# Attention on one Trainium2 core: the projections of a batch moved nearer to its scores, and the small steps around them reordered

## The reference

```python
x = x + tanh(g_xattn[0]) * xattn(layernorm(x), ctx, Wq, Wk, Wv)
x = x + tanh(g_ffn[0]) * ffn(layernorm(x), ...)

def xattn(x, context, Wq, Wk, Wv):
    q = x @ Wq.T;  k_raw = context @ Wk.T;  v_raw = context @ Wv.T
    kv = concat([k_raw, v_raw], -1).reshape(b, m, 32, 16, 2)
    q, k = rmsnorm(q), rmsnorm(kv[..., 0]);  v = kv[..., 1]
    return softmax(q @ k.T * 16 ** -0.5) @ v

def ffn(h, ...):
    # one of 8 experts a row (top 1 of x @ router_w.T), gated by a sigmoid,
    # w_gate_up[e] (512 x 2048), silu(g) * u, w_down[e] (1024 x 512),
    # plus one shared expert of the same shapes for all rows
```

## Time and profile before

| | before |
|---|---|
| median of 3 runs | 1104.04 us (1103.55 to 1106.19) |
| the profiled execution, its time | 1103.48 us |
| its span | 1101.4 us |
| mean granted clock of TensorE | 0.977 |
| TensorE busy | 1047.0 us (95%) |
| VectorE busy | 603.8 us (55%) |
| ScalarE busy | 568.7 us (52%) |
| GpSimd busy | 169.3 us (15%) |

### The profile page before, as it was taken

How to read it: one execution, slowest core, us unless ns; L and a number is a source line. 1 busy time by engine, 2 the same in 40 slices (tenths; PEclk the granted TensorE clock), 3 DMA queues, 4 the chain that set the end, 5 groups by cost and what they waited for, 6 DMA issues and landing times. The chain is left out here.

```text
span 1101.4 us, 26510 instructions
## 1 busy us (share of the span) xinstructions
PE 1047.0 (95%) x11645; PEld 852.4 (77%) x11645; DVE 603.8 (55%) x1187; ACT 568.7 (52%) x862; POOL 169.3 (15%) x170
## 2 busy tenths in 40 slices
PE   4889999999999999999669999999999999999997
PEld 3667777777777777776458788888888999999996
DVE  4774455644446554553447644434447666666663
ACT  4356766766676676667543221212125555555552
POOL 0000111101111111111322220000011212333111
PEclk9999999999999999999669999999999999999999
DMA  7400000000000000000113120101038777787762
GB/s 231 104 8 29 30 29 29 30 20 11 29 30 29 29 29 29 2 2 2 43 32 126 50 69 20 39 20 36 15 119 247 233 219 232 231 233 221 214 206 77
DMA packets 62170, 93.14 MB, mean 85 GB/s; under 512 B 5378, under 2 KB 43266, under 8 KB 62048
## 3 DMA queue, kind: packets, MB, share of 16 engines
q1 hardware_dynamic: 53544, 74.90, 22.4%
q0 software_dynamic: 5664, 13.18, 3.9%
q10 hardware_dynamic: 2840, 3.29, 1.0%
HBM read 82.24 MB, written 10.29 MB: 84 GB/s over the span
## 5 line engine op out<-in xcount | busy, mean ns | idle before, releaser
L371 PE MATMUL bank<-arena_f32r 128*128 128x512 f32 (+2 forms) x1344 | 367.5, 411 | 16.7 <-DVE arena_f32r L692 16.6
L371 PEld LDWEIGHTS bank<-arena_f32r 128*128 128x128 f32 (+2 forms) x1344 | 228.4, 182 | 76.0 <-DVE arena_f32r L692 11.4
L584 ACT ACTIVATE probs<-score_banks 128x1600 f32<-128x1600 f32 x96 | 144.7, 1507 | 81.6 <-PE score_banks L407 81.6
L1141 ACT ACTIVATE hT_hi<-arena_f 128x224 fp32r<-128x224 f32 (+1 forms) x96 | 42.2, 440 | 165.7 <-DVE arena_f L1148 165.7
L736 POOL TENSOR_TENSOR k_pack<-normed,k_pack 128x512 f16<-128x512 f32 (+1 forms) x45 | 52.5, 1166 | 417.2 <-ACT k_pack L566 417.2
L706 DVE TENSOR_REDUCE sumsq<-arena_f 128x32 f32<-128x512 f32 (+1 forms) x64 | 43.8, 684 | 132.7 <-ACT arena_f L536 132.7
L422 PE MATMUL bank<-probs,values 128*17 128x100 f32 (+1 forms) x3072 | 89.2, 259 | 10.8 <-ACT probs L584 10.8
L422 PEld LDWEIGHTS bank<-probs,values 128*17 128x17 f32 (+1 forms) x3072 | 65.7, 100 | 43.3 <-issue 30.6
L1123 PE MATMUL bank<-arena_f32r 128*128 128x224 f32 (+1 forms) x672 | 93.6, 298 | 0.8 <-DVE heads_out L751 0.8
L1123 PEld LDWEIGHTS bank<-arena_f32r 128*128 128x128 f32 x672 | 91.1, 193 | 2.4 <-DVE heads_out L751 1.2
L1148 DVE TENSOR_TENSOR arena_f<-bank,arena_f 128x224 f32<-128x224 f32 (+1 forms) x96 | 43.1, 449 | 76.1 <-PE bank L1123 76.1
(11 more groups left out here) (176 smaller groups left out, 1819.3 us busy)
## 6 DMA issues: line engine op xcount, KB each, us to landing
arena_f<-L_ffn_w_gate_up SPq DMA_DIRECT2D x32, 512.0 KB, 4.6
w_raw<-L_ffn_w_gate_up SPq DMA_DIRECT2D x32, 512.0 KB, 4.2
arena_f<-ctx SPq DMA_DIRECT2D x15, 722.0 KB, 4.2
w_raw<-L_ffn_w_down SPq DMA_DIRECT2D x16, 512.0 KB, 4.5
arena_f<-L_ffn_w_down SPq DMA_DIRECT2D x16, 512.0 KB, 3.9
x_all<-x SPq DMA_DIRECT2D x4, 800.0 KB
gated_rows<-arena_f POOLq DMA_DIRECT2D x16, 200.0 KB, 3.6
x_rows<-x_all ACTq DMA_DIRECT2D x4, 800.0 KB
```

Source lines behind the costliest of these rows:

```text
L371: product = PE.matmul(bank[0:rows, :], k.srcT[t % 2][a][:, j, 0:rows], weight, start=(m == 0), stop=(m == 11))
L584: A.activation(k.probs[n % 2][:], k.score_banks[:, :, 0:GH * k.N].rearrange("p j (r n) -> p j r n", r=GH), ACT.Exp, scale=float(HD) ** -0. ...
L1141: A.activation(k.hT[it % 2][0][:, j, 0:width], k.hidden[j][:, 0:width], ACT.Copy).then_inc(r.h_high, 1)
```

## The change

It does these things:

- A batch's projections begin at slot 24 * (b - 2) + 15 (`prep_start`) in place of 24 * (b - 2). Two places replace the one of before: j counts from the start of a batch's projections (up to 40 slots), i from the start of its scores (also up to 40). The slots begin at -41.
- Queries are the fifth product of the seven; the last two are values and keys of the third context tile. The tiles therefore have a new order, 0, 1, 3, 2 (`PLACE`, `TILE`).
- The inverse roots are computed in three groups: context tiles 0 and 1 together, queries, tile 2, at j = 16, 19 and 27, each in the same 11 instructions on 64, 32 and 32 columns.
- The eight turning events of bank 0 stand three slots apart: in slots (modulo 24) 0 x source, 3 pack of tile 2, 6 and 9 the output halves of the batch before, 12 and 15 packs of tiles 0 and 1, 18 and 21 the query halves. The outputs of a batch are so turned 6 and 9 slots after its last row has begun; those of the last batch at 14 and 27.
- Weighted values stand one slot later (`PV_SLOT` = 3), so behind the next unit's scores. Scores need four of the five turned packs, all five only for tile 2.
- The low part of the packs is POOL's for the first batch too.
- x is loaded and normalised in five parts, of batches 0, 1 to 3, 4 to 7, 8 to 11 and 12 to 15; x of batch 0 is the first transfer of SP. The layer norm of the first part is worked off at once; the others stand at slots -14, 4, 28 and 52. The chunks of x1 stand at 96 * (c + 1) + 12 (the last at + 6).
- The routing of the first chunk begins at slot 361 in place of 355.

```diff
-SRC_SLOTS = (-3, 0, 9, 17)
-WEIGHT_SLOTS = (-55, -48, -47, -47, -40, -39)
-RMS_SLOT = 25
-PACK_SLOTS = (6, 8, 11, 14)
-PACK_T_SLOTS = ((9,), (11,), (15,), (19, 21))
-PV_SLOT = 2
-OUT_SLOTS = (13, 25)
-X1_SLOT = 8
+LEAD = 15
+PLACE = (0, 1, 3, 2)
+TILE = (0, 1, 3, 2)
+VALUE_AT = (0, 2, 5)
+HEADS_AT = (1, 3, 6, 4)
+PROJECTION_TILE = (0, 0, 1, 1, 3, 2, 2)
+SRC_SLOTS = (-3, 0, 9, 13)
+WEIGHT_SLOTS = (-7, 0, 1, 1, 12, 13)
+RMS_SLOTS = (16, 19, 27)
+RMS_TILES = (slice(0, 2), slice(3, 4), slice(2, 3))
+RMS_OF = (0, 0, 2, 1)
+PACK_SLOTS = (18, 20, 31, 22)
+PACK_T_SLOTS = ((21,), (24,), (36,), (27, 30))
+PACK_T_AT = (0, 1, 4, 2)
+PV_SLOT = 3
+X_PARTS = ((0, 1), (1, 4), (4, 8), (8, 12), (12, 16))
+X_SLOTS = (None, -14, 4, 28, 52)
+ROUTE_SLOT = 361
...
-def windows(k, s):
-    return [(it, s - 24 * it) for it in (s // 24 - 1, s // 24, s // 24 + 1) if -2 <= it < k.B]
+def preparing(k, s):
+    return [(b, s - prep_start(b)) for b in range(k.B) if -4 <= s - prep_start(b) < 40]
+
+def prep_start(b):
+    return 24 * (b - 2) + LEAD
+
+def out_slots(k, b):
+    return (30, 33) if b + 1 < k.B else (14, 27)
+
+def scoring(k, s):
+    return [(b, s - 24 * b) for b in range(k.B) if 0 <= s - 24 * b < 40]
...
 def taken_slot(i):
-    return max(projection_end(i) + 1, PACK_SLOTS[0] + 1) if i == 1 else projection_end(i) + 1
+    return projection_end(i) + 1
...
 def pe_attention(k):
...
+        for b, j in preparing(k, s):
+            if j == SRC_SLOTS[2]:
+                pe_turn_source(k, PE, w, b)
+            for n in range(84):
+                if n * 24 // 84 == j:
+                    pe_project(k, PE, w, b, n)
+            for t in range(4):
+                for half in range(len(PACK_T_SLOTS[t])):
+                    if j == PACK_T_SLOTS[t][half]:
+                        pe_turn_pack(k, PE, w, b, t, half)
+        for b, i in scoring(k, s):
+            for z in range(2):
+                if i == out_slots(k, b)[z]:
+                    pe_turn_outputs(k, PE, w, b, z)
+            for u in range(6):
+                if i == 4 * u + PV_SLOT:
+                    pe_weighted_values(k, PE, w, b, u // 3, u % 3)
...
 def pe_scores(k, PE, w, s):
-    w.wait_ge(k.kt_copied, 5 * b + 5)
+    w.wait_ge(k.kt_copied, 5 * b + (5 if t == k.NMT - 1 else 4))
...
 def dve_attention(k):
...
+        for c in range(len(X_PARTS)):
+            if c:
+                dve_layer_norm(k, V, w, 0, c, s - X_SLOTS[c])
+            elif s == k.first_slot:
+                for step in range(CT + 2):
+                    dve_layer_norm(k, V, w, 0, 0, step)
+        for b, j in preparing(k, s):
+            for p in range(4):
+                if j == SRC_SLOTS[p] + 2:
+                    dve_source_low(k, V, w, b, TILE[p])
+            if j == SRC_SLOTS[2] - 2:
+                dve_normalise_x(k, V, w, b)
+            for n in range(7):
+                if j == taken_slot(n) + 1 and n not in VALUE_AT:
+                    dve_sum_squares(k, V, w, b, PROJECTION_TILE[n])
+            for g in range(3):
+                if j == RMS_SLOTS[g]:
+                    dve_rms(k, V, w, b, g)
+            for t in range(4):
+                if j == PACK_SLOTS[t]:
+                    dve_scale(k, V, w, b, t)
+        for b, i in scoring(k, s):
+            for z in range(2):
+                dve_finish(k, V, w, b, z, i - out_slots(k, b)[z] - 1)
...
-def dve_rms(k, V, w, b):
-    s = k.sumsq[b % 2][:]
-    before = RMS_EVENTS * b
-    w.wait_ge(k.summed, 4 * b + 4)
+def dve_rms(k, V, w, b, g):
+    tiles = RMS_TILES[g]
+    s, root, tmp = (t[:, tiles, :] for t in (k.sumsq[b % 2], k.rms[b % 2], k.rms_tmp))
+    before = RMS_EVENTS * (3 * b + g)
+    w.wait_ge(k.summed, 4 * b + 2 + g)
     V.tensor_scalar(s, s, 1.0 / HD, RMS_EPS, MULT, ADD).then_inc(k.rms_v, 1)
-    w.wait_ge(k.scaled, 4 * (b - 2) + 4)
+    w.wait_ge(k.scaled, 4 * (b - 2) + 2 + g)
     for step in range(RSQRT_STEPS):
         w.wait_ge(k.rms_v, before + step + 1)
-        rsqrt_step(V, k.rms[b % 2][:], k.rms_tmp[:], s, step).then_inc(k.rms_v, 1)
+        rsqrt_step(V, root, tmp, s, step).then_inc(k.rms_v, 1)
...
 def sp_attention(k):
     SP, w = k.SP, Waits(k.SP)
+    sp_load_x(k, SP, 0)
     sp_load_weights(k, SP, w, 0, 0)
...
     sp_load_context(k, SP, w, 0, slice(1, None))
-    sp_load_x(k, SP, 0)
     for half in range(2):
         sp_load_weights(k, SP, w, 2, half)
-    for b in range(1, k.B):
+    sp_load_context(k, SP, w, 1)
+    for c in range(1, len(X_PARTS)):
+        sp_load_x(k, SP, c)
+    for b in range(2, k.B):
         sp_load_context(k, SP, w, b)
```

More of the change, by code:

```diff
@@ L30 @@
 RSQRT_STEPS = 10
-LN_EVENTS = 2 * 4 + 1 + RSQRT_STEPS
 RMS_EVENTS = 1 + RSQRT_STEPS
@@ L201, in lay_out_semaphores @@
 def lay_out_semaphores(k, sem):
-    k.x_in = [sem(f"x_in{i}") for i in range(4)]
+    k.x_in = [sem(f"x_in{i}") for i in range(len(X_PARTS))]
     k.ctx_in = [sem(f"ctx_in{i}") for i in ("_even", "_odd", "_rest")]
@@ L279, in turn_order @@
     for s in range(k.first_slot, k.last_slot):
[L280 to L284, removed]
+        for b, j in preparing(k, s):
+            order += [("src", b)] if j == SRC_SLOTS[2] else []
+            order += [("pack", b, t, half) for t in range(4) for half in range(len(PACK_T_SLOTS[t]))
+                      if j == PACK_T_SLOTS[t][half]]
+        for b, i in scoring(k, s):
+            order += [("out", b, z) for z in range(2) if i == out_slots(k, b)[z]]
     return order, {name: n for n, name in enumerate(order)}
@@ L305, in pe_attention @@
             pe_scores(k, PE, w, s + 1)
[L306 to L325, removed]
+        for b, j in preparing(k, s):
[15 more added lines that the diff above has]
+                    pe_weighted_values(k, PE, w, b, u // 3, u % 3)
+        if s == ROUTE_SLOT - 1:
             pe_turn_router(k, PE, w)
-        if 355 <= s < 355 + ROUTE_STEPS:
-            pe_route(k, PE, w, 0, s - 355)
+        if 0 <= s - ROUTE_SLOT < ROUTE_STEPS:
+            pe_route(k, PE, w, 0, s - ROUTE_SLOT)
     return w
@@ L477, in act_attention @@
-        if s == 354:
+        for b, j in preparing(k, s):
+            for p in range(4):
+                if j == SRC_SLOTS[p] + 1:
+                    act_source_high(k, A, w, b, TILE[p])
+            for n in range(7):
+                if j == taken_slot(n):
+                    if n in VALUE_AT:
+                        act_copy_values(k, A, w, b, PROJECTION_TILE[n])
+                    else:
+                        act_take_heads(k, A, w, b, PROJECTION_TILE[n])
+            for t in range(4):
+                if j == PACK_SLOTS[t] + 1:
+                    act_pack_high(k, A, w, b, t)
+                for half in range(len(PACK_T_SLOTS[t])):
+                    if j == PACK_T_SLOTS[t][half] + 1:
+                        act_copy_pack(k, A, w, b, t, half)
@@ L483, in act_attention @@
+        if 0 <= s - ROUTE_SLOT - ROUTE_STEPS < 2:
+            act_part_high(k, k.first, A, w, s - ROUTE_SLOT - ROUTE_STEPS)
     return w
@@ L661, in dve_weight_low, with ln_part, ln_done, dve_layer_norm @@
     V.tensor_tensor(low, src, high.bitcast(F32), SUB).then_inc(k.w_low, 1)
[L664 to L668 removed]
+def ln_part(x1, c):
+    return (CT * c, CT * c + CT) if x1 else X_PARTS[c]
+def ln_done(x1, c):
+    done = 0
+    for at in [(0, i) for i in range(len(X_PARTS))] + [(1, i) for i in range(4)]:
+        first, end = ln_part(*at)
+        done += 2 * (end - first) + 1 + RSQRT_STEPS
+        if at == (x1, c):
+            return done
+def dve_layer_norm(k, V, w, x1, c, step):
+    first, end = ln_part(x1, c)
+    before = ln_done(x1, c) - 1 - RSQRT_STEPS
+    if 0 <= step < end - first:
         if x1:
[L670 removed]
+            w.wait_ge(k.x1_made, 2 * end)
         else:
             w.wait_ge(k.x_in[c], 16)
[L673 to L674 removed]
+        V.bn_stats(k.ln_raw[:, first + step, :], k.x_all[:, first + step, :]).then_inc(k.ln_v, 1)
+    part = slice(first, end)
     if step == CT:
[L676 to L677 removed]
+        w.wait_ge(k.ln_v, before - (end - first))
+        for b in range(first, end):
             V.bn_aggr(k.ln_mv[:, b, :], k.ln_raw[:, b, :]).then_inc(k.ln_v, 1)
[L679 removed]
+        w.wait_ge(k.ln_v, before)
         V.tensor_scalar(k.ln_var[:, part], k.ln_mv[:, part, 1], LN_EPS, None, ADD).then_inc(k.ln_v, 1)
[L681 to L682 removed]
     if step == CT + 1:
[L684 to L685 removed]
+        for i in range(RSQRT_STEPS):
+            w.wait_ge(k.ln_v, before + 1 + i)
             rsqrt_step(V, k.ln_rstd[:, part], k.ln_tmp[:, part], k.ln_var[:, part], i).then_inc(k.ln_v, 1)
@@ L690, in dve_source_low @@
     src, high, low = source_views(k, b, t)
-    w.wait_ge(k.src_high, 4 * b + t + 1)
+    w.wait_ge(k.src_high, 4 * b + PLACE[t] + 1)
     V.tensor_tensor(low, src, high.bitcast(F32), SUB).then_inc(k.src_low, 1)
 def dve_normalise_x(k, V, w, b):
-    w.wait_ge(k.ln_v, LN_EVENTS * (b // CT + 1))
+    w.wait_ge(k.ln_v, ln_done(0, [c for c, (first, end) in enumerate(X_PARTS) if first <= b < end][0]))
     w.wait_ge(k.src_turned, b)
```

201 lines of the change are left out of this document (71 added, 130 removed).

## The result

The changed kernel takes 1121.36 us (median of 4 runs, 1119.9 to 1124.58), the kernel before 1105.12 in the same series (1103.55 to 1106.65). The ratio is 1.0151 with a 95% interval of 1.0121 to 1.0181: 16 us slower. Forecast were 1108.5 in a range of 1078 to 1118, so the side was right and the size was not: the time lies 3.4 us above the range. The profiled execution took 1122.42 us with a span of 1120.5.

What follows compares the result with a forecast made beforehand. PE was taken as full in the middle, idle at both ends. 46 + 469.0 + 18.2 + 9.6 + 3.5 + 1.2 + 34 = 581.5 against 577.03 at the shared stage, 4.5 later, gave 1108.5 us; range 1078 to 1118.

Steps and rivals of the forecast that it cites:

- the moved weighted values: Full middle on PE: operand changes from the new place cost 0, bounds -0.1 and +0.2 us a unit over 88 units.
- the rival: Middle: the clock falls in many batches or operand changes cost 0.1 us a unit, 7 to 10 us more; chance 0.12.
- The queue on DVE: Middle: DVE's work ahead of reading the second output half makes PE wait 1.3 us a batch, 18.2 over 14 batches.
- the straight line: DVE root steps, interpolated between 4 and 128 columns: 0.25 us on 64 columns, 0.22 on 32.
- the held step: Second root group on DVE: POOL's low-part pack of tile 0 holds one root step, 1.0 us more.
- half: Middle: POOL held in place of DVE, or queue 0.8 shorter; 0.5 us a batch, 1095 to 1098 us; chance 0.2.
- the queue fits: Middle: DVE's queue ends before 10.4 us, so turning tile 0 waits for nothing; 1084 us; chance 0.28.
- Layer norms and the clock: First batches: three x layer norm parts in DVE's queue cost 9.6 us, one fall of PE's clock 3.5.
- The chunks of x1: Slots 12 to 17: 0.7 us ahead of the scale of queries for three batches, taken as 1.2 us.
- The start: Up to the first scores: they come at 46 us in place of 63.9, with about 5 us of waiting.
- The tail: Slot 351 to the shared stage: 8 units left, 34 us, bounds 30 and 42.
- weighted values beside the exponential: Tail: weighted values no longer between the exponential and the next scores, 6.5 us less over 8 units.

Runs made afterwards that it cites:

- e8: Changed kernel with four steps in place of ten in each group of norm roots (roots less exact): 1086.83 us, ratio 0.9843.
- e11: Changed kernel with four root steps in place of ten, weighted values issued right behind their slot's scores, ahead of its projections: 1072.58 us.
- e9: Changed kernel with PV_SLOT back at 2, x layer norms at slots 17, 41 and 65, and four root steps in place of ten: 1073.91 us.
- e5: Changed kernel with PV_SLOT back at 2 and the last x layer norms at slots 17, 41 and 65: 1095.55 us.
- e3: Changed kernel with the root group of queries at j = 21 in place of 19: 1121.3 us.
- e6: Changed kernel with PV_SLOT 2, x layer norms at 17, 41 and 65, and the root group of queries at 21: 1100.87 us.
- e7: Changed kernel with VectorE's scoring steps, the readers of the turned output, ahead of the preparing steps of the same slot: 1121.19 us.
- e4: Changed kernel with the last three x layer norm parts at slots 17, 41 and 65 in place of 4, 28 and 52: 1113.07 us.
- e1: Changed kernel with weighted values back in slot 4u + 2, directly ahead of the next unit's scores: 1108.11 us.
- e2: Kernel before with only the weighted values moved to slot 4u + 3, behind the next unit's scores: 1116.93 us.
- e10: Kernel before with four steps in place of ten for its norm roots, as a control: 1097.45 us.
- e12: Changed kernel with PV_SLOT 2, x layer norms at 17, 41 and 65, and seven root steps in place of ten: 1084.06 us.

## Why the prediction was right or wrong

**The step that failed: the moved weighted values, taken as 0.** The prediction bounded it at -0.1 and +0.2 us a unit and took 0 "because the wait for the exponential moves with it". In the full middle there was no such wait to move. Measured are 1.14 to 1.16 us a period, 0.19 a unit (e8 against e11 and e9), at the upper bound: 88 units, 16.9 us. The sentence ahead of it had the reason why no value between the bounds was supported: no row showed weighted values followed by a projection. With the upper end the forecast would have been 1126; the bound was kept out of the range by giving operand changes a share of a chance of 0.12 and sizing them at 0.1 in the rival.

**The queue on DVE: right.** 1.3 us a batch were forecast. Taking the queue's load away won 1.07 (e8 against after) and 1.22 (e9 against e5). The root steps cost 0.25 and 0.22 as on the straight line, the held step 0.9 in place of 1.0. Seen as a wait of PE it is only 0.74 a period, because PE itself came later to it. That POOL's pack would hold DVE and not the reverse held in these rows, and "half" and "the queue fits" fell with it. The text summed the whole queue but put the wait at its one reader, the second output half; e3, e6 and e7 show that another order earns nothing, since the next thing in line is as late.

**Layer norms and the clock: right in kind.** 9.6 + 3.5 = 13.1 forecast; e4 took 11.6 us out of the three periods. The clock fell with a wait of 3.4 us as forecast (0.89 from 96 to 128 us), and once more with one of 3.3 (0.95 from 128 to 160), where the forecast had one fall. The chunks of x1 cost 0.87 in three periods, 2.6 us in place of 1.2.

**The start: right.** 46 forecast, 45.61 measured, with 4.2 us of waits for POOL's pack where 5 were taken.

**The tail: 34 forecast, 39.1 measured.** Its step of 8 x 0.81 = 6.5 us, weighted values beside the exponential, cannot be found in the runs. With the weighted values away from the scores the tail is shorter in three pairs, by 1.7 (e1, 40.8 against 39.1), 2.4 (e9, 38.2 against e8, 35.8) and 1.4 (before, 41.4, against e2, 40.0), but longer by 4.7 in the fourth (e5, 36.1, against e4, 40.8). e5 and e6 lie 6.0 apart with one group of roots moved, most of it with the clock. So the tail scatters by as much as the effect, and how the 5.1 us divide stays open. The window of the tail after has PE busy for 28.99 of 40 us at a clock of 0.73:

```profile
554.00:594.00 40.00, 28.99 (x646) 22.74 (x645) 20.87 (x66) 22.51 (x29) 13.70 (x25) 0.73 0.17 51
```

Its largest waits are 2.3 us for a copied output and 1.8 for a copied pack, both of ACT. What each of its waits and the clock cost was not tried.

**The sum.** Against the forecast of the shared stage at 581.5 it came at 593.38, 11.9 later: -0.4 at the start, +7.2 from the first scores to unit 88 (508.7 in place of 469.0 + 18.2 + 9.6 + 3.5 + 1.2 = 501.5), +5.1 in the tail. The middle's +7.2 hides larger parts: +16.9 for the cut projections; -4.4 for what is left of the period (33.9 less 1.15 and 1.07 is 31.68, 0.30 below the 31.98 that the forecast used, 14.7 times); -2.5 for the queue (1.07 taken 14.7 times is 15.7, not 18.2); -2.8 because the first period is that much shorter than a steady one (31.08 against 33.9 in e4); -1.5 for the layer norms of x and +1.4 for those of x1. They give 7.1. Behind the seam come 2.7 us for which the forecast had nothing. (The forecast's own arithmetic is a little loose in two rivals: 581.5 - 18.2 - 3.5 - 2 is 557.8, which gives 1085 and not 1084, and "half" gives 1094 to 1097; neither moves the range.)

**Its own tests.** The successor of L387 waited for that of L751 12 times by 500 us, most by 0.74 and not 1.2; the period was 33.9, not 33.3; batches came longer by 3 to 5 us. The forecast of 33.3 missed by just the operand changes, less what the new order wins.

## What to carry to other kernels

Where TensorE is full, an issue order that puts another kind of matmul between two small ones cost 0.19 us in every unit here though no view showed a wait: compare the spacing of starts, or the period, not the busy share. When a wait names the last reader of a buffer on a full queue, first shorten the queue or move work out of that stretch; a new order gives the wait another name. And where a term has no row, and the bounds times their count decide the sign, the range has to hold the worse bound together with the other costs, not in place of them.

## What the hardware showed that was not expected

Matmuls with nothing changed but their neighbours took longer: 14 projections took 3.53 us in two pieces around the weighted values and 3.34 in one piece, PE being busy at full clock in both. With the earlier trace rows alone that cannot be seen.

The same wait brought the clock down in some executions and not in others. From the shared stage's start to the end of the span before took 524.4 us and after 527.1, with the same work. 1.3 of the 2.7 are in its first 24 matmuls. The rest is in a second fall, 60 to 80 us into the stage, before and after:

```profile
637.03:657.03 20.00, 18.25 (x104) 16.50 (x104) 11.28 (x33) 3.54 (x6) 6.45 (x8) 1.00 0.30 94
653.38:673.38 20.00, 18.26 (x96) 16.30 (x95) 11.34 (x33) 3.98 (x7) 6.46 (x8) 0.91 0.23 69
```

In both PE waits 1.7 us there for VectorE; behind that wait the clock fell only in the changed kernel. The fourteen profiles divide by this fall: without it (before, e3, e8, e10, e11, e12) the stage took 524.3 to 524.4 us, with it 525.9 to 527.9. It isn't the entry alone: e2 had its first 24 matmuls in 4.64 us, the shortest, had the fall and took 525.9. What decides whether the clock falls, no run shows.

A small step on VectorE (0.19 us) with two operands in SBUF, beginning 0.12 us behind a pack of POOL, was held until that pack's end (1.09 us), once in each batch. The Trainium skill says in SBUF — State Buffer, section "Who interferes with whom", that the order of issue decides who blocks; POOL began 0.12 us earlier in these rows, and the trace agrees.
